# Batch 0's head projection moved into the first fp6 layer, and scaled values kept in the centred ones' place

## The reference

```python
x = x + 0.5 * moe(layernorm(x))          # 16 experts, 4 of them per token, 2 shared
x = x + attention(layernorm(x))          # one wide head
x = x + 0.5 * moe(layernorm(x))
x = x + 0.5 * fp6_linear(layernorm(x))
x = x + heads(layernorm(x))              # 16 heads, causal, relative bias
x = x + 0.5 * fp6_linear(layernorm(x))
```

```python
scales = max(max(abs(blocks), axis=-1) / 7.5, eps)
q = nearest_on_grid(blocks / scales[..., None], GRID)
out = (q * scales) @ (wq * ws).T + bias
```

```python
x0 = x; xn = layernorm(x) * gamma + beta
q, k, v = (xn @ W.T for W in (Wq, Wk, Wv))     # 16 heads of 16
y = softmax(q @ k.T / 4 + bias, causal) @ v
return x0 + y @ Wo.T                            # added to x once more by the caller
```

## Time and profile before

| | us |
|---|---|
| median of 3 runs | 2647.62 |
| lowest and highest | 2645.24, 2648.01 |
| the profiled execution | 2637.26 |
| its span, first to last instruction | 2635.5 |
| mean granted TensorE clock | 0.893 of full speed |
| first fp6 layer, heads, second fp6 layer (about) | 1490 to 1649, 1649 to 2511, 2511 to 2635 |

### The profile page before, as it was taken

The page is one execution under the profiler, slowest core; times in us unless marked ns, Lnnn a source line. Parts: engine busy times, 40 slices in busy tenths (PEclk is TensorE's granted clock), DMA queues, the critical chain, the costliest instruction groups (busy, mean ns, idle before and its releaser), DMA issues.

```text
span 2635.5 us, 39524 instructions
## 1 busy us (share of the span) xinstructions
PE 2158.5 (82%) x13274; PEld 1585.0 (60%) x13274; DVE 1534.9 (58%) x4416; ACT 981.1 (37%) x1967; POOL 315.1 (12%) x306
## 2 busy tenths in 40 slices
PE   4489999957999866999999067468998998999946
PEld 2378888846788735888888046324444444444435
DVE  6744444456555566443433787266875776778287
ACT  4122333323333332233222142324555555555532
POOL 4330000040000035000000510412002002000000
PEclk8699999979999977999999565669999999999966
DMA  7120111020000032111110310253233233231001
GB/s 240 42 72 24 30 29 30 27 70 15 1 1 1 16 97 74 36 30 29 29 30 25 90 32 0 58 63 73 27 50 68 33 50 73 35 41 27 2 24 48
DMA packets 84041, 114.89 MB, mean 44 GB/s; under 512 B 12213, under 2 KB 73817, under 8 KB 80729
## 3 DMA queue, kind: packets, MB, share of 16 engines
q1 hardware_dynamic: 77416, 94.80, 16.4%
q0 software_dynamic: 6432, 17.57, 2.1%
HBM read 69.16 MB, written 43.17 MB: 43 GB/s over the span
## 4 chain that ended last, share of the span: by engine, by line
PE 65%; DVE 19%; ACT 5%; issue 4%; DMA 3%; POOL 2%; POOLq 0%; SPq 0%; ACTq 0%; DVEq 0%
PE psum L778 10%; PE psum L779 9%; PE psum L780 9%; PE psum L122 5%; PE psum L2165 5%; PE psum L123 4%; PE psum L124 4%; PE psum L2144 4%; PE psum L865 3%; PE psum L2124 3%; PE psum L2148 3%; DVE junk L2029 2%; DVE m L2017 1%; DVE xn L180 1%; DMA qk_scr<-parts 1%
## 5 line engine op out<-in xcount | busy, mean ns | idle before, releaser
L1966 ACT ACTIVATE pt<-psum 128x512 f32<-128x512 f32 (+3 forms) x768 | 338.7, 491 | 285.7 <-DVE psum L2055 197.2
L743 DVE SCALAR_TENSOR_TENSOR h<-psum,xg,sg 128x128 f32<-128x128 f32 x592 | 166.9, 344 | 415.8 <-PE psum L865 415.7
L552 ACT ACTIVATE sg<-psum 128x512 f32<-128x512 f32 x180 | 107.4, 597 | 573.3 <-PE psum L780 573.3
L778 PE MATMUL psum<-w_hi,xt_hi 128*128 (+1 forms) x720 | 286.6, 398 | 32.6 <-DVE xt_lo L708 32.6
L779 PE MATMUL psum<-w_lo,xt_hi 128*128 (+1 forms) x720 | 284.0, 394 | 0.0
L780 PE MATMUL psum<-w_hi,xt_lo 128*128 (+1 forms) x720 | 283.0, 393 | 0.0
L2124 PE MATMUL psum<-ks,qs 96*128 96x512 bf16 (+3 forms) x768 | 233.0, 342 | 51.1 <-DMA ks<-qk_scr 20.6
L2144 PE MATMUL psum<-qs,ks 99*128 99x512 bf16 (+3 forms) x768 | 237.6, 332 | 18.6 <-ACT pt L1966 11.6
L778 PE MATMUL psum<-w_hi,ht_hi 128*128 (+1 forms) x720 | 220.1, 306 | 0.2
L2029 DVE CUSTOM_DVE_ANT_0 junk<-psum,band_q 128x256 bf16<-128x256 f32 (+1 forms) x512 | 204.4, 399 | 21.7 <-PE psum L2124 11.6
L780 PE MATMUL psum<-w_hi,ht_lo 128*128 (+1 forms) x720 | 204.8, 284 | 0.0
(11 more groups left out here) (289 smaller groups left out, 4479.4 us busy)
## 6 DMA issues: line engine op xcount, KB each, us to landing
xg<-w_dram SPq DMA_DIRECT2D x54, 256.0 KB, 3.3
qk_scr<-parts SPq DMA_DIRECT2D x32, 384.0 KB, 2.5
qs<-qk_scr SPq DMA_DIRECT2D x96, 128.0 KB, 7.1
ks<-qk_scr SPq DMA_DIRECT2D x96, 128.0 KB, 7.8
xg<-rows_in SPq DMA_DIRECT2D x74, 132.0 KB, 2.2
rows_out<-yb SPq DMA_DIRECT2D x74, 128.0 KB, 1.7
x<-x_dram SPq DMA_DIRECT2D x4, 1024.0 KB, 9.4
out_dram<-x SPq DMA_DIRECT2D x4, 1024.0 KB, 4.4
```

The lines of the kernel that those rows point to most:

```text
L743: ins = dve.scalar_tensor_tensor(out=h[i % 2][:, e, :], in0=u[:, e, :], scalar=xg[j % XSLOT][:, at:at + 1], in1=sg[i % 2][:, e, :], op0=AL ...
L778: pe.matmul(out, a[0], b[0], start=first, stop=False)
L1966: act.activation(pt[n % NPT][:, 0:q1 - q0], st_bank(n)[:, 0:q1 - q0], ACT.Exp).then_inc(*exped.up())
```

## The change

- The projection becomes a class, `HeadProjection`, with its buffers outside the stages, and its steps (`steps(0)`) follow the tables' in the first fp6 layer's `beside`. The first normalisation's statistics of batch 0's 8 tiles are worked out there too (`moments`, `root`, `rsqrt`, on the slice `FIRST`). `linear` takes a tuple of such parts and asks each in turn, on every engine.
- The heads' stage works out the remaining 24 tiles' statistics (`LATER`) and starts with the loads. Semaphores of the projection keep their counts over the barrier (`kept`). The other batches' projections are placed as before.
- In both fp6 layers the scaled values are written over the centred ones, so centre of quad c waits, on ACT, for the turns of quad c - 4 (VectorE's scaled waited for them before, and centre for quad c - 4's scaled). The turned buffers are four in place of eight.

```diff
-    def next_stage(self):
-        for s in self.named.values():
-            s.base = s.total
+    def next_stage(self, kept=()):
+        for name, s in self.named.items():
+            if name not in kept:
+                s.base = s.total
...
-        TILES, QUADS = 2, 4
+        TILES, QUADS, XTS = 2, 4, 4
...
-        def linear(final, tables=None):
-            order = linear_order(final, tables.order() if tables else iter(()))
+        def linear(final, besides=()):
+            order = linear_order(final, (step for part in besides for step in part.order()))
...
-                        self.v, self.e, self.ulp = (sb(st, s, [P, nb, BLK])[:, :, :] for s in ("scaled", "power", "ulp"))
+                        self.e, self.ulp = (sb(st, s, [P, nb, BLK])[:, :, :] for s in ("power", "ulp"))
                         self.xm = source or sb(st, "centred", [P, tiles, D])
-                        self.xt = [] if source else [split(st, "xt", [P, KD, TILES * P]) for _ in range(2)]
+                        self.v = blocks_of(self.xm)
...
+                xts = [split(st, "xt", [P, KD, TILES * P]) for _ in range(XTS)]
...
                             if c >= QUADS:
-                                act.wait_ge(*scaled_ok(c - QUADS + first))
+                                act.wait_ge(*turned(2 * (c - QUADS) + 2))
...
-                            if c >= 2 * QUADS:
-                                act.wait_ge(*lin(c - 2 * QUADS + 1))
+                            if c >= XTS:
+                                act.wait_ge(*lin(c - XTS + 1))
...
                         elif kind == "scaled":
-                            if c >= QUADS:
-                                dve.wait_ge(*turned(2 * (c - QUADS) + 2))
-                            dve.tensor_tensor(q.v, blocks_of(q.xm), wide(q.inv), ALU.mult).then_inc(*scaled_ok.up())
+                            dve.tensor_tensor(q.v, q.v, wide(q.inv), ALU.mult).then_inc(*scaled_ok.up())
...
+        class HeadProjection:
...
+            def order(self):
+                yield [("moments", 1)]
+                for n in (2, 3):
+                    yield [("root", n)]
+                    yield [("rsqrt", n)]
+                yield from self.steps(0)
...
+            def on_dve(self, kind, i, ring):
+                at, parts, rests = self.FIRST, self.parts, self.rests
+                if kind == "moments":
+                    dve_variance(at)
+                elif kind == "rsqrt":
+                    dve_rsqrt(at, i, rstd if i == 2 else rstd2)
+                    if i == 2:
+                        second_variance(at)
+                elif kind == "norm":
+                    if i:
+                        dve.wait_ge(*self.turned(KD * i))
+                    norm(i, self.xn)
+                elif kind == "qk":
+                    bc, n, o, (w, scale) = self.qk_of(i)
+                    if n == 0:
+                        dve.wait_ge(*self.xt_lo(KD * bc + o + 1))
+                    else:
+                        dve.wait_ge(*self.part2(i - KD + 1))
+                    dve.wait_ge(*self.part0(i + 1))
+                    dve.scalar_tensor_tensor(out=rests[o][:, :], in0=ring.bank((kind, i)), scalar=scale,
+                                             in1=parts[:, 0, o, :], op0=ALU.mult,
+                                             op1=ALU.subtract).then_inc(*self.rest_ok.up())
...
-            order = sum(project(0), []) + [("load", u) for u in range(min(NR, NHG))]
+            order = [("load", u) for u in range(min(NR, NHG))]
...
-                    dve_variance(EVERY)
-                    dve_rsqrt(EVERY, 1, rstd)
...
+                    dve_variance(LATER)
+                    dve_rsqrt(LATER, 1, rstd)
+                    second_variance(LATER)
+                    dve_rsqrt(LATER, 2, rstd2)
...
-            linear(False, tables)
-            attention_heads(tables)
+            ahead = HeadProjection(stack, tables)
+            linear(False, (tables, ahead))
+            attention_heads(tables, ahead)
```

More of the change, by code:

```diff
@@ L150, in end_of_stage @@
                 e.wait_ge(*done.now())
-            S.next_stage()
+            S.next_stage(kept)
         def collect(t0, n):
@@ L1280, in emptied @@
                     return wt_lo(i + 1)
-                if kind in ("flip", "flip_turn"):
-                    return tables.emptied(use)
+                for part in besides:
+                    if kind in part.USES:
+                        return part.emptied(use)
                 return (xt_lo if kind == "turn" else lin_x)(i + 1)
@@ L1320, in on_sp @@
                     for kind, c in order:
-                        if tables:
-                            tables.on_sp(kind, c)
+                        for part in besides:
+                            part.on_sp(kind, c)
                         if kind == "w_keep":
@@ L1346, in on_pool @@
                     for kind, c in order:
-                        if tables:
-                            tables.on_pool(kind, c, ring)
+                        for part in besides:
+                            part.on_pool(kind, c, ring)
                 def on_act():
@@ L1389, in on_dve @@
                     for kind, c in order:
+                        for part in besides:
+                            part.on_dve(kind, c, ring)
                         q = of(c) if kind in ("amax", "scaled", "power", "less", "last_bit", "shift", "even", "requant") else None
@@ L1463, in on_pe @@
                     for kind, c in order:
-                        if tables:
-                            tables.on_pe(kind, c, clear)
+                        for part in besides:
+                            part.on_pe(kind, c, clear)
                         if kind == "w_turn":
@@ L1504, in linear @@
                 on_pe()
-                end_of_stage("linear")
+                end_of_stage("linear", [name for part in besides for name in part.KEPT])
         class HeadTables:
@@ L1659, in macaron, with second_variance @@
+        def second_variance(at):
+            then(dve.tensor_tensor(ve[:, at], mv[:, at, 1], rstd[:, at], ALU.mult))
+            then(dve.tensor_tensor(ve[:, at], ve[:, at], rstd[:, at], ALU.mult))
+            dve.tensor_scalar(ve[:, at], ve[:, at], LN_EPS, None, ALU.add).then_inc(*S("variance").up())
         CELLS = [(0, 0), (0, 1), (1, 0), (4, 1), (1, 1), (2, 0), (5, 1), (2, 1), (3, 0), (6, 1), (3, 1), (7, 1)]
@@ L1673, in spans, with heads_order @@
             return w, bw, far, min(far, BANK) if w > BANK else 0
[L1675 to L1687, removed]
+        def heads_order(project):
             def maxima(u):
@@ L1775, in heads_order, with attention_heads @@
             return order + sum(tail, [])
-        def attention_heads(tables):
-            order = heads_order()
+        def attention_heads(tables, ahead):
+            order = heads_order(ahead.steps)
             nth = {}
@@ L1855, in on_sp @@
                     for kind, i in order:
[L1856 to L1865 removed]
+                        if kind == "qk" and i % (2 * KD * CB) == 0 and i // (2 * KD * CB) >= 2:
+                            b = i // (2 * KD * CB)
+                            for u in range((b - 1) * NHG - NR, (b - 1) * NHG):
+                                sp.wait_ge(*stacks_of(u % NR, u))
+                        ahead.on_sp(kind, i)
+                        if kind == "load":
                             b, g = divmod(i, NHG)
@@ L1958, in on_act @@
+                        if kind == "v" and i // (2 * CB) >= 2:
+                            act.wait_ge(*value((i // (2 * CB) - 1) * NHG * NCELL))
+                        ahead.on_act(kind, i, mx_ring)
+                        if kind == "score":
                             n, j, c, h, q0, q1, b1 = cell_of(i)
@@ L1996, in on_dve @@
                     for kind, i in order:
[L1997 to L2011 removed]
+                        ahead.on_dve(kind, i, mx_ring)
+                        if kind == "max_zero":
                             dve.wait_ge(*max_zero(i + 1))
```

305 lines of the change are left out of this document (161 added, 144 removed).

## The result

The changed kernel took 2622.58 us (median of 4 runs, 2618.07 to 2628.48), and the kernel before, beside it, 2646.43 us (4 runs, 2643.22 to 2648.01). The ratio is 0.9913, with a 95% interval of 0.989 to 0.9936. The longer series of the first experiment gives a ratio of 0.9919 [0.9906, 0.9932], 20.3 us.

A forecast was written before the change was run, and what follows sets the result against it. The projection behind the first fp6 layer was taken as a chain of hand-overs, no engine busy half the time. Terms -11.0 - 2 + 0.3 = -12.7 us, from a median of 2647.62 to 2635.0 us, range 2625 to 2643.

The forecast's parts named there:

- the clock term: TensorE's clock at the first fp6 layer's end: may rise for quad 7's products and qk, 0 to -5.6 us, taken as -2.
- Chunk 0 and prelude, -11.0: Projection's chunk 0 and statistics prelude overlap the first fp6 layer: first load at 1697.0 instead of 1708.0, 11.0 us won.
- A page's rule: TensorE's slow clock is released by activity; by it -5.6 us would come in full, so it got a chance only.
- POOL beside VectorE, +0.3: POOL's add slows VectorE's elementwise steps in the first fp6 layer: 0 to +1 us, taken as +0.3.
- In-place values, four buffers, 0: Both fp6 layers: scaled values over centred ones and four turned buffers instead of eight cost 0 us.
- Nothing overlaps: Rival: chunk 0 paid in full in the layer, only the prelude won, -2.3 us, 2645.3; little overlap or loads held: 0.12.
- The clock rises for quad 7's products: Rival: products 14 and 15 take near 4 us together, -16.6 us, 2631.0; clock rises or more won: 0.17.
- Slower: Rival: TensorE's clock is lost in the heads' stage, +7 us at 40 us of slowed matmuls, 2655; chance 0.09.

The follow-up runs named there:

- the first experiment: The changed kernel again, no edit, in more rounds: 2624.33 us (6 runs) against 2644.6 for the kernel before (17 runs), ratio 0.9919.
- Experiment 3: The changed kernel with two empty rounds behind qk 0, so qk 1 and 2 follow quad 7's products: 2631.45 us, ratio 0.9952.
- experiment 5: The kernel before with twelve throwaway matmuls ahead of products 14 and 15 of the first fp6 layer: 2672.04 us against 2672.12, ratio 0.9994.
- experiment 2: The kernel before with only scaled values in the centred ones' place and four turned buffers: 2642.79 us, ratio 0.9994.
- experiment 1: The changed kernel run again without any edit, against the kernel before: 2624.33 us (6 runs), ratio 0.9919.

## Why the time came out lower than predicted

The step that failed is the clock term: "Since the layer's products kept the low level for long, I take -2." The whole bound of 5.6 came. The prediction's own landmarks, with those of the changed kernel moved by the 1.26 us of sum 9 (the predicted ones are without the clock term):

| | predicted | measured | difference |
|---|---|---|---|
| products 12 begin | 1629.9 | 1629.4 | -0.5 |
| turn of chunk 0 | 1638.1 | 1637.5 | -0.6 |
| qk 0 | 1643.4 | 1642.5 | -0.9 |
| first rest | 1647.1 | 1646.2 | -0.9 |
| products 14 begin | 1652.8 | 1651.2 | -1.6 |
| qk 3 (products 15 are through) | 1661.1 | 1655.9 | -5.2 |
| norm 1 | 1668.8 | 1662.2 | -6.6 |
| first load | 1697.0 | 1691.0 | -6.0 |

- **Chunk 0 and prelude, -11.0: right.** Down to the first rest each step is within 0.9 us: the two sums as a pair, norm 0 (1.38 against 1.24), the products, the stall (7.70 against "over 8"). Norm 1 beside an idle POOL took 1.38 and not 2.21, -0.83 against -0.97. From norm 1 to the first load it is 28.78 against 28.17.
- **The clock, -2: mis-sized; it measured -5.7.** The rows between qk 0 and norm 1 take the difference from -0.9 to -6.6, so 5.7 us, where the bound was 5.6: products 14 and 15 4.7 instead of 8.2, qk 3 1.4 (1654.63 to 1656.04) instead of 2.6, and most of the rest within qk 1 and 2. Experiment 3 takes two qk away from in front of the products, and 8.2 us and the low level are back; experiment 5 puts other matmuls in front of them in the kernel before, and they take 4.85. The error was in the argument from the layer's slices. Those at 0.50 with TensorE busy throughout show at what level these products ran that time, and not at what level they run when the clock has risen ahead of them. Nor do they show that such products can't raise it: in the same profile of the kernel before, the last layer's quads 6 and 7, with the same instructions and nothing else on TensorE, ran at the high level.
- **A page's rule.** That activity releases the slow clock (the Trainium skill, "TensorE: Matmul & The Clock Gate", section "What's actually happening") agrees with the changed kernel's 1.00 in the window from 1650 to 1655, and with experiment 5. The 5 busy microseconds at 0.50 in the earlier trace rows and in experiment 3 still stand beside it, so the rule alone did not give the level of a single group here.
- **POOL beside VectorE, +0.3: right.** Beside the add of chunk 0, "last bit" took 0.92 instead of 0.69: +0.23.
- **In-place values, four buffers, 0: right**, by experiment 2.
- **Rivals.** "Nothing overlaps" fell: norm 1 is 11 us ahead of the 1673 from which it decides. "The clock rises for quad 7's products" is what happened. It said -16.6 us, and the first part shows -16.5 (-16.8 in experiment 1); its 2631.0 for the whole kernel is above what was measured, for the reasons below. "Slower" did not come: from the first load to the maxima it is 15.70 us against 15.46, and the heads are not longer (784.62 and 786.74 against 788.05).

The clock term alone does not bring the time out of the range: with -5.7 in place of -2 the sum is -16.4, and the forecast would have been 2631.2. The rest goes like this. The first part's 16.5 are most of the 20.3 us of the longer series. The heads of the changed kernel are without the fall of the clock at some 85 us, 135.0 - 132.2 = 2.8 us, which the prediction had as a risk of the other sign; that it comes and goes with timing is shown, and that all runs of the two kernels stand as their profiles do is only argued (over the whole stage the heads were 3.4 us shorter in one profile and 1.3 in the other). The sum, 19.3, is inside the interval of the first experiment (0.9906 to 0.9932: 18 to 25 us), and so would be the 18.1 of experiment 1's own profile (16.8 and 1.3). By the longer series' 20.3 us the time beside 2646.43 would have been 2626, inside the range; that the first four runs gave 23.9 and 2622.58, outside it, is in part scatter. The profiled execution of the kernel before lay 9 to 10 us under its median, and some 2 to 6 of these are its last layer, the shortest of its kind (123.99; the others without extra matmuls there 126 to 130), by the clock of quads 6 and 7.

## What to carry to other kernels

A matmul's duration depends on the clock that is granted while it runs, so a step that is moved in front of a product group can change the group's price by over 40% (8.2 to 4.7 us), and a busy share of 100% at the low level does not say that the work would stay there. One group at one level in one profile says little: look at the same group in several profiles, and at its like in other stages. Where a stage's matmuls come in short groups behind waits, look at the granted clock of the group itself, and try dense throwaway matmuls in the wait ahead of it: it paid where the group is on the path that sets the end (the last layer, 126 to 114 us), and little where another engine is full and the extras ended 5 us ahead of the products (the first). When a chain is laid beside another, list the queue of each engine in the new order, as the stall of 7.70 us could be read before it was there.

## What the runs showed of the hardware

The same products of quad 7 took 8.2 us behind a wait of 1.9 or 2.6 us, 4.7 behind qk 1 and 2, and 4.85 behind twelve bf16 matmuls of 512 columns. The granted level also came and went with small shifts in time: 7 us once behind the same wait of 1.9, and in the last layer, with the same steps, anything from neither to both of the last two groups at the high level, worth 124 to 130 us.

The prelude of the other 24 tiles, which now lies beside POOL's setting of ones, has three steps of 0.18 us that took over ten times as long. The timeline of POOL and VectorE in the changed kernel:

```profile
1687.66 10.63 POOL L2060 MEMSET ks<- 3x4096 bf16 x3
...
1688.77 2.43 DVE L176 TENSOR_SCALAR newton<-newton 128x24 f32<-128x24 f32 x1
...
1691.45 0.18 DVE L1847 TENSOR_TENSOR var_eps<-mean_var,rstd 128x24 f32<-128x24 f32 x1
...
1691.89 2.88 DVE L1849 TENSOR_SCALAR var_eps<-var_eps 128x24 f32<-128x24 f32 x1
...
1695.06 0.30 DVE L173 RECIPROCAL recip<-std 128x24 f32<-128x24 f32 x1 [0.29 <-ACT std L169]
...
1695.83 2.50 DVE L176 TENSOR_SCALAR newton<-newton 128x24 f32<-128x24 f32 x1
```

The three TENSOR_SCALAR instructions ended within 0.04 us of a memset's end (the three memsets take 10.63 us, 3.54 each, and so end at 1691.20, 1694.75 and 1698.29). A TENSOR_TENSOR, with two tensor operands, took 0.18 beside the same memsets, and a RECIPROCAL, with one, its usual 0.30. The Trainium skill ("SBUF — State Buffer", section "SBUF: two separate sides") calls the port pair of VectorE and GpSimd an exclusive lock that is held for the whole instruction. It lets a VectorE operation of two inputs collide only with a GpSimd operation that reads, and one of a single input only when it runs in a mode that takes both ports. The ends at the memsets' ends and the TENSOR_TENSOR agree with this; in which mode the TENSOR_SCALARs and the RECIPROCAL ran no row shows. Here it costs nothing, since VectorE is next needed at 1706.10; the prediction had this prelude as covered, at an uncovered price of 5.7 us, and beside POOL that price would have been some 7 us higher (2.43 + 2.88 + 2.50 less three times 0.18).
